# Three attention stages without a projection phase: the projections of a batch run among the steps of the batch before it

## What is computed

```
x = x + attention(layernorm(x), ctx)
v, k, q = ctx @ Wv.T + bv, ctx @ Wk.T + bk, layernorm(x) @ Wq.T + bq
qk   = einsum('nqhd,nkhd->nhqk', q, k)
qk   = where(mask == 0, 1e-20, qk)             # attention 0 alone
attn = softmax(qk / sqrt(E), axis=3)
out  = einsum('nhqk,nkhd->nqhd', attn, v) @ Wo.T + bo
```

## Time and profile before

| | us |
|---|---|
| median of 3 executions | 5331.87 (5326.46 to 5332.09) |
| the profiled execution | 5328.68 |
| its span in the trace | 5327.0 |
| PE / DVE / ACT / POOL busy | 4330.9 / 3321.3 / 2128.3 / 809.1 |
| projection phases of `a0_`, `a2_`, `a3_` | 164.4, 154.7, 156.6 |

### The profile page before, as it was taken

How to read it: one execution, slowest core, us unless ns; L and a number is a source line. 1 busy time by engine, 2 the same in 40 slices (tenths; PEclk the granted TensorE clock), 3 DMA queues, 4 the chain that set the end, 5 groups by cost and what they waited for, 6 DMA issues and landing times. The chain is left out here.

```text
span 5327.0 us, 86304 instructions
## 1 busy us (share of the span) xinstructions
PE 4330.9 (81%) x31716; PEld 3113.2 (58%) x31716; DVE 3321.3 (62%) x7267; ACT 2128.3 (40%) x3668; POOL 809.1 (15%) x478
## 2 busy tenths in 40 slices
PE   5699995999766999795478888559997897699888
PEld 4344444777655777674367777544554666355566
DVE  6566653444475666544855544458885887688576
ACT  2255552222112333342033333226775673477510
POOL 4423310000051000000012222310001233100000
PEclk8799997999877999897579999778997888799888
DMA  6222211000021000010034433441210004222000
GB/s 205 71 75 67 75 33 43 1 0 0 23 87 33 16 16 16 24 42 29 0 118 105 109 100 98 123 154 57 65 52 17 0 0 152 73 66 67 30 16 16
DMA packets 171769, 302.70 MB, mean 57 GB/s; under 512 B 22556, under 2 KB 90830, under 8 KB 171480
## 3 DMA queue, kind: packets, MB, share of 16 engines
q1 hardware_dynamic: 158824, 280.59, 16.7%
q0 software_dynamic: 12672, 18.42, 1.8%
HBM read 216.60 MB, written 80.77 MB: 56 GB/s over the span
## 5 line engine op out<-in xcount | busy, mean ns | idle before, releaser
L1552 ACT ACTIVATE a_pT<-a_psS 128x512 f32<-128x512 f32 x1536 | 836.0, 597 | 398.0 <-PE a_psS L1438 392.7
L1624 DVE TENSOR_REDUCE a_mx<-a_psA 128x1 f32<-128x512 f32 x1024 | 656.5, 685 | 82.3 <-PE a_psA L1416 82.2
L1416 PE MATMUL a_psA<-a_ks,a_qs 48*128 48x512 f32 (+1 forms) x1536 | 403.9, 521 | 156.9 <-PEq L46 93.7
L1453 PE MATMUL a_psZ<-a_pT,a_V 128*17 128x128 f32 x12288 | 488.1, 278 | 0.0
L1620 DVE CUSTOM_DVE_ANT_0 a_scored<-a_psA,a_hide_q 128x512 bf16<-128x512 f32 x512 | 332.7, 688 | 190.6 <-PE a_psA L1416 189.6
L1453 PEld LDWEIGHTS a_psZ<-a_pT,a_V 128*17 128x17 f32 x12288 | 272.6, 97 | 271.7 <-issue 158.5
L1416 PEld LDWEIGHTS a_psA<-a_ks,a_qs 48*128 48x128 f32 (+1 forms) x1536 | 151.0, 191 | 403.9 <-issue 174.6
L1438 PE MATMUL a_psS<-a_qs,a_ks 50*128 50x512 f32 (+1 forms) x1536 | 317.9, 407 | 2.8 <-ACT a_pT L1552 0.8
L2894 DVE SCALAR_TENSOR_TENSOR ex_h<-ex_psU,ex_ub,ex_sg 128x512 f32<-128x512 f32 x129 | 96.9, 751 | 318.3 <-PE ex_psU L159 311.3
L740 DVE TENSOR_TENSOR m_h_l<-m_h,m_h_h 128x512 fp32r<-128x512 f32 x64 | 44.3, 693 | 267.6 <-ACT m_h_h L684 265.5
L157 PE MATMUL m_psH<-m_xe_h,m_w_h 128*128 128x512 f32 x512 | 210.7, 411 | 0.0
(11 more groups left out here) (554 smaller groups left out, 11198.4 us busy)
## 6 DMA issues: line engine op xcount, KB each, us to landing
a_k_parts<-a_p_kp SPq DMA_DIRECT2D x96, 256.0 KB
a_q_parts<-a_p_qp SPq DMA_DIRECT2D x96, 256.0 KB
a_qs<-a_q_parts SPq DMA_DIRECT2D x192, 128.0 KB
a_ks<-a_k_parts SPq DMA_DIRECT2D x192, 128.0 KB
X<-in_L_ffn_gw SPq DMA_DIRECT2D x36, 512.0 KB
X<-in_L_ffn_up_w SPq DMA_DIRECT2D x36, 512.0 KB, 3.6
X<-in_L_ffn_down_w SPq DMA_DIRECT2D x36, 512.0 KB, 3.8
a_p_cT<-in_ctxT SPq DMA_DIRECT2D x24, 512.0 KB, 7.4
```

The costliest lines, as they stand in the source:

```text
L1416: nc.tensor.matmul(psA[:, unit(a, par) % 3], qs[r, g % ring, p % 2, q * P:(q + 1) * P], ks[r, g % ring, p % 2], start=True, stop=True).the ...
L1453: last = nc.tensor.matmul(psZ[q * VP:q * VP + VW, g % 2, j * P:(j + 1) * P], V[:, b, kt, g % NG * GH + j, :], pT[:, p % 2, par, kt, q * P: ...
L1552: nc.scalar.activation(pT[:, p % 2, par, kt, :], psS[:, unit(t, par) % 3], ACT.Exp).then_inc(exp_done, 1)
L1624: nc.vector.tensor_reduce(mx[:, p // 2 % 2, par, p % 2, q:q + 1], psA[:, unit(a, par) % 3], AX_X, ALU.max).then_inc(a_used, 1)
```

## The change

`resident_projections` and `Prepare` are gone, and with them the barrier. The table `found` has the projections as items: for a batch that begins at step c, "xT" (normalised x turned) at c-55 and c-45, "part" (a half of K's or Q's columns: 6 matmuls of 512 columns) at c-42, -39, -37, -34, and "values" (12 matmuls of 256) at c-25 and c-22. The steps begin at -60; before -16 only such items run. DVE does a batch's `statistics` at c-59 and `normalise` at c-57, ACT its root at c-58. "turn" and "out" come later (c+38 to c+49), an "out" in one step. Buffers are shared or cut: V holds 2 batches, the context and `on` one, the parts two halves; `osb` lies in `oh`, the raw weights in `pT`, and in attention 0 `oraw` in `scored` and `lower_half` in `xn`. Number of ACT_TABLE_LOAD rows in the whole program: 48 before, 84 after (a group of instructions counts as a row).

```diff
-        V = sb("V", [P, B, TB, H, VW])
+        V = sb("V", [P, VRING, TB, H, VW])
...
+            c = SPAN * u
+            found += [(c + 38, "turn", KD * u), (c + 43, "turn", KD * u + 1), (c + 46, "out", 2 * u), (c + 49, "out", 2 * u + 1)]
+            found += [(c - 55, "xT", KD * u), (c - 45, "xT", KD * u + 1), (c - 42, "part", 4 * u), (c - 39, "part", 4 * u + 1),
+                      (c - 37, "part", 4 * u + 2), (c - 34, "part", 4 * u + 3), (c - 25, "values", 2 * u), (c - 22, "values", 2 * u + 1)]
...
+                            if n >= 2:
+                                act.wait_ge(part_stored[n % 2], 32 * (n // 2))
...
+                    if r == -58 and 0 < u < B:
+                        roots(u)
...
+                    if u > 0 and hidden is not None:
+                        dve.wait_ge(least_ready, u)
+                    for q in range(TB):
+                        last = nc.vector.tensor_scalar(xn[:, q, :], G.X[:, u * TB + q, :], meanvar[:, q, 0:1], rstd[:, q:q + 1],
+                                                       ALU.subtract, ALU.mult)
...
+                    if 0 <= a < QUARTERS:
+                        maximum(a, 0)
+                    for what, n, k in ending(t - 1, "xT", "part", "values"):
+                        projected(what, n, k)
+                    if 0 <= a < QUARTERS:
+                        maximum(a, 1)
...
+                    u, r = (t + 60) // SPAN, (t + 60) % SPAN - 60
+                    if r == -51 and 0 < u < B:
+                        context_low(u)
+                    if hidden is not None and 0 <= u < B:
+                        if r == -40:
+                            query_mask(pool, u)
+                        if r == -38:
+                            least_maximum(pool, u)
+                    u, r = (t + 26) // SPAN, (t + 26) % SPAN - 26
+                    if hidden is not None and 0 <= u < B:
+                        if r == -26:
+                            key_mask(pool, u)
+                        if r == -24:
+                            key_hide(pool, u)
+                    u, r = (t - 40) // SPAN, (t - 40) % SPAN
```

More of the change, by code:

```diff
@@ L1365, in attention_by_pairs @@
-        if hidden is not None:
-            for u in range(B):
-                found += [(H * KD * u + 4 * q - 10, H * KD * u + 4 * q - 10, "sums", TB * u + q) for q in range(TB)]
-        found.sort()
-        number = {(what, n): k for k, (_, _, what, n) in enumerate(found)}
-        steps = range(-LEAD, found[-1][1] + 2)
-        def ending(t, *whats):
-            return [(what, n, k) for k, (_, last, what, n) in enumerate(found) if last == t and what in whats]
-        def bank(t):
-            return psZ[:, (t - STEPS - TB) // STEPS % 2]
@@ L1445, in values @@
                     if p % 2 == 0 and i == 0:
-                        before = sum(1 for _, last, _, _ in found if last < t)
+                        before = sum(1 for last, _, _ in found if last < t)
                         pe.wait_ge(x_free, before)
@@ L1581, in take_output @@
                     dve.wait_ge(x_full, k + 1)
+                    if u > 0 and g % NG == 0:
+                        dve.wait_ge(x_full, number["turn", KD * u - 1] + 1)
                     got = bank_of(k).rearrange("p (j q v) -> p j q v", j=GH, v=VP)
+                    normal = on[:].rearrange("p q (h d) -> p h q d", h=H)[:, heads]
                     if hidden is not None:
@@ new lines, in _ @@
+                statistics(0)
+                nc.vector.memset(nparts[:].bitcast(F32), 0.0).then_inc(chain, 1)
+                nc.vector.memset(psZ[:], 0.0).then_inc(z_set, 1)
+                normalise(0)
+                for count, n in enumerate(names):
+                    weight_low(n, count)
+                dve.wait_ge(small_loaded, 16 * 5)
+                nc.vector.tensor_scalar(bqs[:], bq[:], q_scale, None, ALU.mult).then_inc(scaled, 1)
+                nc.vector.memset(V[:, :, :, :, DH:VW], 1.0)
@@ L1655, in _ @@
-                add_output(2 * B - 2)
-                add_output(2 * B - 1)
+                    nc.gpsimd.tensor_tensor(tiles, tiles, osb.rearrange("p (q d) -> p q d", q=2), ALU.add).then_inc(out_added, 1)
+                set_ones(0)
+                context_low(0)
+                for slot in range(1, ring):
+                    set_ones(slot)
+                if hidden is not None:
+                    nc.gpsimd.memset(score_bias[:], score).then_inc(stacks_set, 1)
+                    pool.wait_ge(stacks_set, 4 * ring + 1)
```

658 lines of the change are left out of this document (312 added, 346 removed).

## The result

The changed kernel takes 5426.97 us (median of 4 executions, 5413.68 to 5435.73), the kernel before 5331.98 in the same comparison: the ratio is 1.0175, with a 95% interval of 1.0147 to 1.0202. It is slower by some 95 us. The profiled execution, the fastest of the four, is 5413.68 us and stands 85 us above the one of before.

What follows compares the result with a forecast made beforehand. In the steps PE and DVE are nearly full, while the projection phases waste time on stores and a low clock. `a0_` +19.7, `a2_` -7.7, `a3_` -9.6 sum to +2.4 us on 5331.9: 5334 us, range 5270 to 5392.

Steps and rivals of the forecast that it cites:

- three signs: Wrong if POOL's masks lie elsewhere in time, the granted clock stays under 0.9 in the steps, or prologue is 20 us longer.
- Prologues: Ahead of the first maximum, replacing the projection phases: 37 us in `a2_` and `a3_` (bounds 27 and 47), 57 in `a0_`.
- Twice the store wait of 4.93 us: Prologue term of 9.9 us for batch 0's stores and the loads of the first stacks, which must follow each other.
- Lead-ins: Steps ahead of the main ones, taking the parts of batch 1: +4.8 us in `a2_` and `a3_`, +5.8 in `a0_`.
- 16 of 18.7 show: Steps of `a2_`, `a3_`: PE's 9.6 plus DVE's 9.1 us a batch, partly covered at about four of nine items.
- Rival 3: Nothing overlaps in the steps and the clock falls: 18.7 us a batch, 5383 us, slower by 1%; chance 0.17.
- PE's items 6.9 us a batch: Steps of `a0_`: DVE has idle time, so its halves cost little; of PE's items 6.9 us a batch count.
- The stall beside POOL: Steps of `a0_`: normalisation on DVE waits for POOL's key mask, copy and bias; 10.8 us a batch with the statistics.
- Table loads: ACT in the steps: two loads of 1.28 us a batch, counted as covered by ACT's idle time.
- rival 5: 42 table loads in the steps, each with a tail as long as itself, on the path: 54 us, 5388 us; chance 0.07.
- rival 4: The stores bind again: two Q parts of ACT wait 3 us each per batch, 108 us, 5440 us; chance 0.09.
- The clock: Drops after new stalls in the steps: 1.5 us a batch, 9 in all, in `a2_` and `a3_`; 2.3 in `a0_`.

Runs made afterwards that it cites:

- Experiment 8: experiment 6 with SyncE issuing the stacks of group 1 only once those of group 0 have landed: 5329.7 us, 1.0001 of the kernel before.
- experiment 5: Changed kernel with the parts of batches 2 to 7 made of high times high alone, 2 of their 6 matmuls: 5387.9 us in one execution.
- experiment 4: Changed kernel without DVE's low halves of K and Q parts for batches 2 to 7: 5403.8 us in one execution.
- experiment 10: experiment 9 with, in `a2_` and `a3_`, second values item at 19 steps ahead (was 22), outputs one step later, context halves two: 5321.3 us, 0.9985 of before.
- experiment 9: experiment 6 with, in `a2_` and `a3_`, parts 42, 38, 34, 30 steps ahead and normalisation behind both maxima of its step: 5324.2 us, 0.9995 of before.
- experiment 6: Changed kernel with statistics of batches 1 to 7 in prologue gaps, one root, normalisation five steps earlier in `a0_` alone: 5328.8 us, 1.0005 of before.
- Experiments 2: Changed kernel with statistics of batches 2 to 7 together ahead of the first maxima and one root for them: 5407.0 us, 1.0137 of the kernel before.
- experiment 3: Changed kernel with a copy of the variance instead of its root for batches 1 to 7, so no table loads among the steps: 5425.7 us, one execution.
- experiment 1: Changed kernel with statistics, root and normalisation of batches 2 to 7 five steps earlier in all three stages: 5398.0 us, 1.0115 of the kernel before.

## Why the prediction was wrong

The forecast was 5334 us, the range up to 5392, the result 5427. None of the three signs that it named for being wrong came: POOL's masks lay where the table had them, the steps ran at 0.94 to 0.98, and the prologues were at most 11 us longer. The steps that failed are two discounts for overlap, the larger in `a0_`, and the stores and loads of the prologue. By the forecast's own steps:

- **Prologues.** 37 us forecast in `a2_` and `a3_`, 46.6 and 47.7 measured: too low by 10 each. Twice the store wait of 4.93 us stood for stores and loads; the stores took 6.4 us, and from the first load issued to PE's scores it was 15.7, while all before the stores took 24.4 of the 27.2 forecast. The upper bound of 47 was about right. Experiment 8 shows that the loads need 9.4 us even by themselves. 57 forecast in `a0_`, 59.8 measured: near, but in part by luck. POOL's masks took 25.3 us and not 20 (33.4 to 58.7), the first two of DVE's normalisations of batch 1 lasted 5.78 us beside them, and items of PE and DVE filled the 9 us behind; the loads, which were too low in `a2_`, ended nothing here.
- **Lead-ins.** 34 and 34.0 in `a2_`: right. 42 and 37.0 in `a0_`: 5 too high.
- **"16 of 18.7 show" in `a2_` and `a3_`.** 18.1 us measured. PE's item adds in full (experiment 5: 3.6 of 3.7 us) and DVE's half adds in full (experiment 4: 2.4 of 2.6), as the turn of the earlier trace rows had said. The step that failed is the discount: a next item was taken to cover DVE's half at four of nine places (the table has eight items). The code has the opposite: `use` waits until all items before are freed, so a neighbour costs 0.6 us of waiting or, where a group opens, 1.1 to 1.2 (trace); moving items apart gave 1.7 us a batch in `a2_` (experiment 10). The wait of 1.14 us at step 20 is in all versions, and no run takes it out. It was in the code, and no price was set on it. One thing was covered that I had not counted so: the normalisation, 1.6, by the sum in experiment 9. 18.7 - 1.6 + 1.7 for neighbours is 18.8, near 18.1; not each of these terms is measured by itself. Rival 3 ("nothing beside") has the size of the batch, but its clock didn't fall in `a2_`, and its 5383 us is 44 short. What hid the miss in part: the steps of `a2_` were 7.9 us over the forecast, +12.3 for six batches and +1.1 for the values of batch 1, less the 9 for the clock that wasn't needed, and +3.5 since the cold start stayed (0.54 in the first 15.2 us of the steps).
- **"PE's items 6.9 us a batch" in `a0_`.** About 14.7 measured (experiment 6). This is the largest miss, near 8 us for each of six batches, and the step that put the result out of the range. 6.9 was less than the forecast's own 9.6 for the same items of PE, without a reason, and DVE's halves stood at nearly nothing because DVE has idle time. Measured, PE's busy time alone rose by 9.8 us, and idle time elsewhere in the batch is no cover: the next item, and the products with V that open a group, wait for DVE's half all the same (5.1 us in experiment 6). The forecast also had no term for the split of the maxima beside POOL's query mask, 1.7 us.
- **The stall beside POOL.** 10.8 us a batch with statistics, 2.3 for the clock, 13.1 together; experiment 6 took 10.6 to 11.2 out. The mechanism and its place were right, and the size within 3 us. Experiments 2 and 3 add what the forecast had not: the stall has a fixed end, that of POOL's run, so whatever is saved ahead of it is lost in it.
- **Table loads.** 1.3 us each, covered by DVE in `a2_` (experiment 3: the batch is 68.3 us either way). The steps have 36 of them and not 42, since batch 1's root comes ahead of the first Exp. The Trainium skill (ScalarE: Activation LUTs, What ACT_TABLE_LOAD costs) has 2.66 us for a switch; no run here shows the drain, and rival 5 is out.
- **Stores (rival 4).** The 24 parts of ACT in the steps of `a2_` waited for PE alone (25.6 us together), none for a store. Out.
- **The clock.** 9 us a stage forecast. In the changed kernel the middle batches of `a2_` ran at 1.00 [windows above], so nothing there; in `a0_` the steps ran at 0.94 instead of 0.99. That none fell in `a2_` and `a3_` is luck: in experiment 4 the clock fell behind the same stall in seven of ten, and in experiment 5 one such fall took 3.8 us.

Together: 46 for the steps of `a0_` (764.7 instead of 719.1), 20 for two prologues and 13 for the steps of `a2_` and `a3_` make 79 of the 83 us between the forecast's span of 5329 and 5412. The account of the items of `a0_` is read from one trace; moving them apart, and the query mask away from the split, was not tried there.

## What to carry to other kernels

Work moved from a half-idle phase into a loop in which two engines hand over to each other at every step cost nearly the sum of what it takes on both here (18.1 of 18.7 us), and not the larger of the two; read what one such item costs today before you give a discount. Price the waits between the moved items themselves, and keep items out of neighbouring steps when each waits for the one before. A stall that ends with another engine's work swallows every saving ahead of it, so remove that first; here statistics ahead of the loop and normalisation away from GpSimd's masks gave back 98 us.

## What the runs showed of the hardware

- VectorE's four normalisations (1.38 us together when POOL was idle, at 3738.00 in experiment 1) took 11.60 us beside GpSimd instructions of 5.37, 5.51 and 2.34 us: they lasted 3.48, 0.40, 5.45 and 2.50 us, three of them ended within 0.2 us behind one of POOL's, and one got in between. In the same kernel the statistics of batch 1, which start at 36.29 us beside POOL's query mask (33.43 to 40.56), took no longer than without it, 0.41 us each.
- Small instructions are held as well: a TENSOR_SCALAR of 128x16, 0.17 us by itself, took 2.37 us beside the query mask (experiment 5), and one of 128x4, as short by itself, 5.31 us in the prologue of experiment 6 (35.08 to 40.39, the mask ended at 40.36).
- A PE wait of 2.11 us in `a2_` left the clock at 1.00 in all middle batches of the changed kernel. In experiment 4 the same wait of 2.11 us at the same step was followed by 0.50 in seven of the ten middle batches of `a2_` and `a3_`, for some 3 to 7 us. So the length of the wait alone doesn't decide it.
- Eight loads of stacks, four of 128 KB and four of 64 KB, landed 9.4 us after the last was issued with none issued behind them; the DMA engines' share was 0.14 in that time, at 52 GB/s (experiment 8, 3462.7 to 3472.0).
